# Expert stage of a fused embedding, state-space and mixture-of-experts layer: the arrivals of up and down weights counted on two semaphores instead of one

## The reference

```python
router_probs = softmax(x @ gate_weight.T)
router_top_value, router_indices = top_k(router_probs, 8)
# four primary experts stay, four secondary ones may be re-routed by a similarity table
combine = sum(one_hot(rerouted_indices, 32) * routing_weights[..., None], axis=1)
def expert_step(y, params):
    wgu, wd, cw = params
    gu = x @ wgu.T
    g, u = split(gu, 2)
    h = silu(g) * u
    y = y + h @ wd.T * cw[:, None]
    return (y, None)
```

## Time and profile before

| what | value |
|---|---|
| median of 3 runs | 2272.41 us |
| lowest, highest | 2266.32, 2274.44 us |
| the profiled execution, own time | 2262.93 us |
| its span, first to last instruction | 2261.2 us |
| PE busy in the span | 1729.0 us, 76% |
| DVE, ACT, POOL busy | 998.1, 750.7, 662.5 us |
| the span outside the expert stage | 1522.65 us |

### The profile page before, as it was taken

The page is one execution under the profiler, slowest core; times in us unless marked ns, Lnnn a source line. Parts: engine busy times, 40 slices in busy tenths (PEclk is TensorE's granted clock), DMA queues, the critical chain, the costliest instruction groups (busy, mean ns, idle before and its releaser), DMA issues. The chain is left out here.

```text
span 2261.2 us, 30323 instructions
## 1 busy us (share of the span) xinstructions
PE 1729.0 (76%) x8941; PEld 1158.9 (51%) x8942; DVE 998.1 (44%) x2295; ACT 750.7 (33%) x1657; POOL 662.5 (29%) x623
## 2 busy tenths in 40 slices
PE   8999997558677584858585867308888888888887
PEld 7999997243536362544445353204444444444443
DVE  5454453153746648293746464412333333333332
ACT  3343433071716344352617071002222222222221
POOL 3112001110024232222223231333444444444443
PEclk9999998777878696968777787559999999999999
DMA  3010002340313121302213130106666566656654
GB/s 122 1 47 10 1 10 80 109 159 0 109 41 90 60 89 34 113 22 78 71 50 99 40 104 1 29 16 175 151 147 137 131 138 139 155 132 148 150 116 85
DMA packets 87376, 191.75 MB, mean 85 GB/s; under 512 B 33791, under 2 KB 38143, under 8 KB 82512
## 3 DMA queue, kind: packets, MB, share of 16 engines
q0 software_dynamic: 36464, 86.90, 17.8%
q1 hardware_dynamic: 50824, 103.68, 14.7%
HBM read 141.21 MB, written 49.32 MB: 84 GB/s over the span
## 5 line engine op out<-in xcount | busy, mean ns | idle before, releaser
L1692 PE MATMUL moe_ps_gu<-moe_wgu,moe_xt 128*128 x944 | 335.6, 499 | 61.9 <-issue 46.7
L1584 POOL DMA_INDIRECT out_h<-moe_yy,moe_idx_s x119 | 187.8, 1578 | 373.0 <-DVE moe_yy L1657 195.6
L1692 PEld LDWEIGHTS moe_ps_gu<-moe_wgu,moe_xt 128*128 128x128 f32 x944 | 170.9, 191 | 181.1 <-issue 88.1
L1682 PE MATMUL moe_ps_y<-moe_wd,moe_ht 96*128 x476 | 229.0, 603 | 12.4 <-issue 10.1
L852 POOL DMA_INDIRECT scratch_slots<-lay_toki,lay_slot x192 | 207.3, 1080 | 82.7 <-issue 58.2
L1130 PE MATMUL lay_ring<-lay_wout,lay_yb 128*128 128x512 f32 x384 | 188.2, 647 | 21.6 <-DVE lay_yb L1350 21.6
L1620 ACT ACTIVATE moe_sl<-moe_ps_gu 128x192 f32<-128x192 f32 x118 | 39.1, 331 | 498.1 <-PE moe_ps_gu L1692 484.8
L1048 PE MATMUL lay_ring<-lay_xnt,win_sb 128*128 128x128 f32 (+2 forms) x1152 | 177.0, 303 | 24.1 <-ACT lay_xa L937 17.7
L1048 PEld LDWEIGHTS lay_ring<-lay_xnt,win_sb 128*128 128x128 f32 (+2 forms) x1152 | 159.7, 211 | 31.1 <-ACT lay_xa L937 20.2
L1086 PE MATMUL lay_ring<-lay_ident,lay_xa 128*128 128x128 f32 (+1 forms) x256 | 54.0, 381 | 156.4 <-ACT lay_xa L924 95.1
L1652 DVE SCALAR_TENSOR_TENSOR moe_hh<-moe_sl,moe_cwv,moe_ps_gu 128x192 f32<-128x192 f32 x118 | 48.9, 414 | 221.3 <-ACT moe_sl L1620 221.3
(11 more groups left out here) (286 smaller groups left out, 2837.9 us busy)
## 6 DMA issues: line engine op xcount, KB each, us to landing
lay_m<-scratch_cum SPq DMA_DIRECT2D x16, 1536.0 KB
moe_wgu<-in_wgu SPq DMA_DIRECT2D x32, 768.0 KB
moe_wd<-in_wd SPq DMA_DIRECT2D x32, 384.0 KB
win_sb<-in_win SPq DMA_DIRECT2D x1, 4384.0 KB, 14.8
scratch_xg<-lay_x SPq DMA_DIRECT2D x16, 272.0 KB, 3.2
tok_u_raw<-in_tok_u SPq DMA_DIRECT2D x16, 256.0 KB, 2.8
tok_v_raw<-in_tok_v SPq DMA_DIRECT2D x16, 256.0 KB, 3.2
lay_m<-scratch_cum SPq DMA_DIRECT2D x16, 256.0 KB
```

Source lines behind the costliest of these rows:

```text
L1584: pool.indirect_dma_start(out=a["out"], out_offset=bass.IndirectOffsetOnAxis(ap=idx_s[n][:, 0:1], axis=0), in_=yy[n][:], in_offset=None, b ...
L1682: last = mm(ps_y[:], ht[:, q], wd[:, bass.ds(r * 2 + q, 1)].rearrange("p o n -> p (o n)"), start=q == 0, stop=q == 1)
L1692: last = mm(ps_gu[n][:], xt[n][:, t], wgu[:, bass.ds(r * KD + t, 1)].rearrange("p o n -> p (o n)"), start=t == 0, stop=t == KD - 1)
```

## The change

`w_in` becomes two semaphores: `up_in`, to which the transfers of `wgu` add, and `down_in`, to which those of `wd` add. Each counts 16 per expert, so the table's field `F_W` is 16 per expert instead of 32. On PE the up product waits for `up_in` alone. `down` reads one more word of the table, `F_W` of its own tile, and waits for `down_in` before it waits for `ht`. SP waits for both where it waited for one.

```diff
-W_DMAS = 2
...
-                own.step(v.tensor_scalar(ff[:, F_W], ef[:], 1.0, float(16 * W_DMAS), ALU.add, ALU.mult))
+                own.step(v.tensor_scalar(ff[:, F_W], ef[:], 1.0, 16.0, ALU.add, ALU.mult))
...
-        w_in = s.sem("w_in")
+        up_in = s.sem("up_in")
+        down_in = s.sem("down_in")
...
-                        sp.wait_ge(w_in, e * (16 * W_DMAS))
+                        sp.wait_ge(up_in, e * 16)
+                        sp.wait_ge(down_in, e * 16)
                         sp.wait_ge(down_pe, room)
-                        sp.dma_start(wgu[:, r * KD:(r + 1) * KD], a["wgu"][bass.ds(e, 1)].rearrange("o p k n -> p (o k) n")).then_inc(w_in, 16)
-                        sp.dma_start(wd[:, r * 2:(r + 1) * 2], a["wd"][bass.ds(e, 1)].rearrange("o p k n -> p (o k) n")).then_inc(w_in, 16)
-                sp.wait_ge(w_in, 16 * W_DMAS * E)
+                        sp.dma_start(wgu[:, r * KD:(r + 1) * KD], a["wgu"][bass.ds(e, 1)].rearrange("o p k n -> p (o k) n")).then_inc(up_in, 16)
+                        sp.dma_start(wd[:, r * 2:(r + 1) * 2], a["wd"][bass.ds(e, 1)].rearrange("o p k n -> p (o k) n")).then_inc(down_in, 16)
+                sp.wait_ge(up_in, 16 * E)
+                sp.wait_ge(down_in, 16 * E)
...
                 def down(t, ht_count):
                     r = entry(pe, F_RING, t, W_RING - 1)
+                    arrivals = entry(pe, F_W, t, 16 * E)
+                    pe.wait_ge(down_in, arrivals)
                     pe.wait_ge(ht_dve, ht_count)
...
-                        arrivals = entry(pe, F_W, i * 2 + n + 1, 16 * W_DMAS * E)
+                        arrivals = entry(pe, F_W, i * 2 + n + 1, 16 * E)
                         r = entry(pe, F_RING, i * 2 + n + 1, W_RING - 1)
-                        pe.wait_ge(w_in, arrivals)
+                        pe.wait_ge(up_in, arrivals)
```

## The result

| | before | changed |
|---|---|---|
| median | 2269.85 us (4 runs, 2266.32 to 2274.44) | 2298.02 us (4 runs, 2292.1 to 2307.53) |
| ratio on record for the comparison | | 1.0129, 95% interval 1.0093 to 1.0164 |
| the profiled execution, own time | 2262.93 us | 2298.06 us |

The change costs 1.3%. The kernel before has one run more here than in the table ahead of the change. The forecast was 2293 with a range of 2279 to 2307.

What follows compares the result with a forecast made beforehand. PE was taken to bound the last stage. One added read of 0.75 us, exposed in 20 to 36 tiles, gave 15 to 27 us, middle 21, other terms 0: 2272.4 + 21 = 2293 us, range 2279 to 2307.

Steps and rivals of the forecast that it cites:

- The wait for the weights, term 0: Ahead of the up product: waits named after down weights, 13.3 us, are not real, so splitting the semaphore gains 0.
- 0.75 us for one more exposed read: On PE's sequencer ahead of the down product: one more table read costs about 0.75 us where not hidden.
- Which tiles pay: Tiles whose weight load waits for a gather pay: 20 to 36 payments, 15 to 27 us, middle 21.
- What comes back in the next gather wait: In the tile after a delayed one the gather wait shrinks, so two neighbours pay 0.75 us together, not 1.5.
- Caught reads: Table reads that start while POOL writes a gather's descriptors take longer: 5 us possible, taken as 0.
- The second wait: The wait on `down_in` ahead of the down product: taken as 0, with 2 us left for the range.
- Absorbed: Rival: the gather chain sets the pace and later gather waits take up the delay; 0 to 8 us, chance 0.15.
- faster: Rival: the 13.3 us ahead of the up product are real waits for down weights and go; 2259 us, chance 0.04.
- Every tile or half of them: Rival: the sequencer's lead does not cover two reads; 88 us for all 118 tiles, 44 for half, chance 0.11.

Runs made afterwards that it cites:

- The read alone: The kernel before plus one unused table read ahead of each down product, semaphore unsplit: 2278.81 us, ratio 1.0104.
- The wait alone: The kernel before plus a second wait at the down product, on a constant long reached, no added read: 2257.97 us, ratio 1.0013.
- second trace: The changed kernel run and profiled once more, unaltered, against the kernel before: 2308.37 us, ratio 1.0129.
- all reads early: The kernel before with all of PE's loop table reads moved under the up product, four in two tiles, words kept in registers: 2260.44 us, ratio 0.9877.

## Why the prediction was right, point by point

- **The wait for the weights, term 0: right.** The gap ahead of the up product stayed at 60 us; with two semaphores the kernel is no faster wherever the reads stand (0.9914 against 0.9913), and the named wait disappears with moved reads and an unsplit semaphore.
- **0.75 us for one more exposed read: right.** Where the first read keeps its common length, the second starts 0.76 us after it in one half of the loop and 0.69 in the other (middle values over the tiles). The late tile at 1548.97 has 1.77 us from transposes to down product, in the forecast's 1.5 to 1.9. So have 12 of the 21 tiles whose weight load waited for a gather; 2 have less, and 7 more, up to 2.33, with a stretched read in each. Reads went from 355 to 474, as forecast. The read alone cost 23.5 us against a forecast of 21. The Trainium skill's floor of 600 ns, which the forecast had weighed ("DMA: Bandwidth & Descriptors", "Latency and other measured facts"), is contradicted again: 304 ns in the middle of 474 reads, 295 at the least.
- **Which tiles pay: mis-sized.** The forecast counted tiles in which the weight load waits for the gather, 36, and set between 20 and 36 payments, 27 us at most. Idle time ahead of the down product grew by 32.2 us, so this was no upper count. In 25 of the 46 tiles with a gap the weight load had not waited for a gather; the tile at 1999.62 is one. The forecast named them ("some tiles that don't wait now have less than 0.75 us of cover") and gave them no number. It also set the cover that two reads need too low, a gather that landed 0.7 us before the up product ends. In the changed kernel tiles whose first read starts 1.2 us ahead of the transposes pay nothing, and those with 0.9 us pay 0.2 to 0.3 us. The trace of the kernel before could have told: in 66 of its tiles the down product's read starts less than 1.1 us ahead of the transposes, the 36 and 30 more.
- **What comes back in the next gather wait: right in kind, and smaller than the cost.** Gather waits of the weight load fell from 30.9 to 15.7 us; on PE itself the return was 5.7 us out of 32.2, and 2.0 more came back ahead of the up product.
- **Caught reads, 0 with 5 in the range: some 6.6 us, taken at 0 too early.** Of the tiles with a gap ahead of the down product, 25 have a read of over 350 ns in the changed kernel and 15 had one before. What these reads took over the common 304 ns, at most the gap of the tile, sums to 12.6 us after and 6.0 before. No run changes the stretching alone, so this is an estimate from the two traces.
- **The second wait, 0 with 2 us in the range: about 3 us in one kernel, 0 in another.** The wait alone gave +0.13% [-0.01, 0.26]; with the added read moved early the whole change came to 1.0001.
- **Missing from the sum: PE's own busy time.** It rose by 9.1 us; in the groups 6.2 of it are the down product's. A down product that follows without a gap takes 1.88 us, and one after a gap, also a gap too short for the views, 1.98. There are 69 of these instead of 42, which makes 2.7 us; another 2.9 us are down products at a lower granted clock (below).
- **The number: right, in part by luck.** The forecast's 21 us were idle time of PE, net of what comes back. The two traces show 24.5 us for that, of which the stretched reads are a part that the forecast had set to nothing, and 9.1 us of busy time that it did not have at all. Only the width of the range, +7 to +34, took these in.
- **The rivals.** Absorbed would have been 0 to 8 us, faster a gain: the ratio's interval, 1.0093 to 1.0164, excludes both. Every tile or half of them, 44 us and more, is excluded too: the tile at 1563.73 is covered.

## What to carry to other kernels

A scalar read on an engine's own sequencer was free in these kernels while it stood under running work, and cost its full length behind a wait; before adding one, or when looking for time, put every such read ahead of the longest wait of the loop (here that alone was worth 20 us; with fewer reads on top it was up to 28, which is not clear of the errors). A wait that the profile names after a transfer may only show the last event: ask which transfer that product needs before splitting a semaphore for it, and count the read that the split brings. When many short gaps go at once, look for the chain that then sets the pace: 71.6 us of gaps went, 69 came back in the wait for the gather, and of the 28 us won the move of one read alone had won 20.

## What the runs showed of the hardware that was not expected

**A table read mostly gets two to three times longer when it starts beside a gather's issue, and not beside a scatter's.** In the kernel before, the rows of the sequencers of DVE and PE from 1903.5 to 1904.5 us, then POOL's timeline:

```profile
L1545 DVEq TENSOR_LOAD <-tile_tab x1: 1094/1094/1094, 1903.5 to 1903.5; - x1
...
L1545 PEldq TENSOR_LOAD <-tile_tab x1: 827/827/827, 1903.9 to 1903.9; - x1
...
1903.19 1.07 POOL L1578 DMA_INDIRECT moe_xg<-scratch_xg,moe_idx_g  x1 [0.30 <-issue]
```

Two engines' reads start during the gather's 1.07 us and both end near 1904.6 to 1904.7, some 0.4 us after it. The read at 1901.4 started during the scatter of 1901.31, which takes POOL 1.58 us, and took 307 ns. Over all of PE's reads it is the same. In the kernel before 62 of the 355 start while POOL issues a gather; 56 of them take over 350 ns, 725 ns in the middle. Of the 53 that start while it issues a scatter none takes over 312. In the changed kernel it is 88 of 96, 714 ns in the middle, and none of 116. In all, 59 reads took over 350 ns before and 94 after. What the two share was not tried.

**After waits PE sometimes comes back at half its clock.** In the changed kernel from 2056 to 2072 us, PE's timeline and then busy times by engine with the granted clock (the third number from the end):

```profile
2056.72 2.84 PE L1697 MATMUL moe_ps_gu<-moe_wgu,moe_xt 128*128 x8 [1.11 <-issue]
2060.72 0.66 PE L1701 MATMUL moe_ps_xt<-moe_ident,moe_xg 128*128 128x128 f32 x4 [1.16 <-DMA moe_xg<-scratch_xg,moe_idx_g]
2062.49 3.78 PE L1687 MATMUL moe_ps_y<-moe_wd,moe_ht 96*128 x4 [1.11 <-DMA moe_wd<-in_wd]
...
2056.00:2062.00 6.00, 3.50 (x12) 1.86 (x12) 1.32 (x6) 0.91 (x2) 2.65 (x2) 1.00 0.96 259
2062.00:2067.00 5.00, 4.51 (x7) 2.13 (x8) 0.69 (x2) 0.00 (x1) 0.00 (x0) 0.54 0.33 90
```

After three waits close together, of 1.11, 1.16 and 1.11 us, the granted clock falls from 1.00 to 0.54, close to the lower of its two levels, 1.2 GHz, and the down product takes 3.78 us instead of 1.98. The same run of waits need not do it: in the tile at 1548.97 they were 0.93, 1.22 and 1.11 us, the granted clock of the next 5 us stayed at 1.00, and the down product took 1.98 us. What decides is not shown. Such slow down products stand 3 times among 118 in the changed kernel, 3.7 us in all over 1.98 each, 6 times in its second trace, and once before the change, 0.8 us. With all reads early they stand 9 times, 10.1 us; one of them, PE's timeline and the busy times around it:

```profile
1895.35 1.11 PE L1706 MATMUL moe_ps_xt<-moe_ident,moe_xg 128*128 128x128 f32 x4 [4.42 <-DMA moe_xg<-scratch_xg,moe_idx_g]
1896.26 3.62 PE L1681 MATMUL moe_ps_y<-moe_wd,moe_ht 96*128 x4
...
1895.00:1900.00 5.00, 4.65 (x10) 2.42 (x11) 0.08 (x1) 1.87 (x2) 0.00 (x0) 0.50 0.54 143
```

Here PE waited 4.42 us for a gather and came back at 0.50. The idle time of PE is nearly the same in this kernel as before the change, but it lies in fewer and longer waits, and the stage runs at a granted clock of 0.97 instead of 1.00. That takes some of the gain away.
